# Attention layer with quantised feed-forward: the mask and the maximum of the scores move from TensorE and a plain reduction to a masked reduction on DVE, and DVE's order within a turn changes

## The reference

```
x = x + layernorm(attention(layernorm(x)))
x = x + layernorm(ffn(layernorm(x)))

attention: 32 query heads of 128, 8 key/value heads (4 query heads share one)
  y     = softmax(mask(rope(q) rope(k)^T / sqrt(128))) v     in blocks of 64 rows, each sees itself and the block before,
                                                             key no more than 64 back; the first block of a sequence sees only itself
  o_lin = gated linear attention: S = S * exp(g_t) + softmax(k)_t v_t^T ;  o_t = softmax(q)_t S ;  g = log_sigmoid(k) / 16
  out   = bf16(0.5 * y + 0.5 * o_lin) Wo
ffn: w1, w2, w3 are first rounded to NF4 (per 64 values: scale by the largest magnitude, round to one of 16 codes, scale back),
     then  (silu(x w1^T) * (x w2^T)) w3^T          with a hidden width of 1376
```

## Time and profile before

| | |
|---|---|
| median of 3 runs | 1959.39 us (1958.69 to 1960.08) |
| the profiled execution, its own time | 1959.31 us |
| its span | 1957.5 us, 42161 instructions |
| busy share of PE, DVE, ACT, POOL | 96%, 73%, 63%, 63% |
| granted clock of PE, mean | 0.99 |
| DMA | 61.43 MB, 31 GB/s over the span |

### The profile page before, as it was taken

One profiled execution on the slowest core, in us unless ns is written; L12 is line 12 of the kernel. 1 busy time (PEld: TensorE's weight loads), 2 busy tenths in 40 slices (PEclk: granted clock), 3 DMA queues, 4 the chain that ended last, 5 costly groups with the idle time before them and its releaser, 6 DMA issues.

```text
span 1957.5 us, 42161 instructions
## 1 busy us (share of the span) xinstructions
PE 1876.3 (96%) x11698; PEld 1252.8 (64%) x11698; DVE 1433.4 (73%) x3926; ACT 1229.4 (63%) x4840; POOL 1235.9 (63%) x1150
## 2 busy tenths in 40 slices
PE   4999999999999999999999999999989979999997
PEld 3667677777777777776777676777666635444443
DVE  6998888888888888888888888888899644302022
ACT  5777777777777777777777777776666535312121
POOL 3777777777777777777777777777677521212121
PEclk8999999999999999999999999999999989999999
DMA  5000000000000000000000000000100042000000
GB/s 199 25 26 25 26 25 24 24 24 24 32 25 24 24 24 24 29 24 24 24 24 24 30 29 24 24 24 13 54 13 7 7 134 79 26 1 22 0 21 21
DMA packets 44353, 61.43 MB, mean 31 GB/s; under 512 B 4928, under 2 KB 18496, under 8 KB 44288
## 3 DMA queue, kind: packets, MB, share of 16 engines
q1 hardware_dynamic: 44288, 60.64, 9.6%
HBM read 47.97 MB, written 12.65 MB: 31 GB/s over the span
## 4 chain that ended last, share of the span: by engine, by line
PE 62%; DVE 16%; issue 14%; POOL 3%; ACT 2%; DVEq 1%; DMA 0%; SPq 0%; POOLq 0%; ACTq 0%
PE bank L1250 18%; PE bank L1239 8%; PE bank L1278 6%; PE bank L1221 4%; PE bank L1294 4%; PE bank L1315 4%; PE bank L1379 3%; PE bank L1287 3%; DVE f_s L963 2%; PE bank L1205 2%; PE bank L1304 2%; POOL hl L527 2%; DVE f_nrm L953 2%; PE bank L1270 1%; PE bank L1297 1%
## 5 line engine op out<-in xcount | busy, mean ns | idle before, releaser
L488 POOL TENSOR_TENSOR f_acc<-f_acc,f_s 128x512 f32<-128x512 f32 (+1 forms) x416 | 534.3, 1284 | 30.6 <-POOL f_acc L488 0.4
L1250 PE MATMUL bank<-wh,xh 128*128 (+2 forms) x1024 | 334.9, 327 | 7.3 <-DVE cumh L1099 6.2
L1250 PE MATMUL bank<-wl,xh 128*128 (+2 forms) x1024 | 335.0, 327 | 0.0
L1250 PE MATMUL bank<-wh,xl 128*128 (+2 forms) x1024 | 334.7, 327 | 0.0
L469 POOL TENSOR_TENSOR pr<-pr,rp 128x512 f32<-128x512 f32 x128 | 133.0, 1039 | 229.5 <-DVE rp L894 229.5
L963 DVE TENSOR_SCALAR f_s<-f_nrm 128x512 f32<-128x512 f32 (+1 forms) x480 | 240.9, 561 | 3.7
L575 ACT ACTIVATE qe<-bank,nqm 128x128 f32<-128x128 f32 x512 | 180.8, 365 | 80.3 <-DVE qs L823 57.2
L527 POOL TENSOR_TENSOR hl<-hf,hh 128x512 f16<-128x512 f32 (+1 forms) x44 | 50.8, 1155 | 283.7 <-ACT hh L754 283.7
L1379 PE MATMUL bank<-xh,w 128*128 (+3 forms) x704 | 224.8, 382 | 3.8 <-ACT sg L748 3.8
L603 ACT ACTIVATE pr<-bank,pmx 128x128 f32<-128x128 f32 x512 | 180.9, 367 | 37.5 <-DVE pmx L887 29.6
L1239 PE MATMUL bank<-wh,oT 128*128 (+1 forms) x512 | 194.0, 379 | 3.8 <-DVE xl L1019 1.4
(11 more groups left out here) (177 smaller groups left out, 4973.7 us busy)
## 6 DMA issues: line engine op xcount, KB each, us to landing
f_raw<-wf SPq DMA_DIRECT2D x30, 256.0 KB, 2.6
dequantised<-f_dq SPq DMA_DIRECT2D x30, 256.0 KB, 2.0
wt<-dequantised SPq DMA_DIRECT2D x30, 256.0 KB, 3.0
raw_qkv<-wq SPq DMA_DIRECT2D x29, 256.0 KB, 2.5
raw_o<-wo SPq DMA_DIRECT2D x29, 256.0 KB, 2.6
rows<-x SPq DMA_DIRECT2D x4, 1024.0 KB, 9.3
xr<-x SPq DMA_DIRECT2D x16, 256.0 KB, 3.6
out<-yo SPq DMA_DIRECT2D x16, 256.0 KB, 2.1
```

The source lines that it names most:

```text
L488: nc.gpsimd.tensor_tensor(f_acc[:, 0:w], f_acc[:, 0:w], f_s[:, k % 8, 0:w], ALU.add)\
L1250: last = nc.tensor.matmul(dst, av, w[:, sl + c, lo:hi], start=(n == 0), stop=(n == 3 * NC - 1))
```

## The change

1. **Mask.** PE's mask matmul goes; the first product of the scores opens the bank. `p_max` on DVE is now a memset of one unused column (`pause`), and for each of the four heads an operation that adds the mask to 128 columns of SC, negates them, writes them back and keeps the minimum in `pmx`. ScalarE's exponential gets `scale=-1`. In p=0 the first two heads take the mask from `win0`, which ScalarE copies once per step (`head_mask`).
2. **State.** `state` is split: the sum stays ahead of `p_max`, the scaling stands behind it. `em` (p=1) is now an exponential on ScalarE.
3. **Order.** `rks` moves from ahead of `kt` to behind `log_decay`. The compares (and `f_nrm`) stand ahead of `gl` in all four p; in p=0 they stood behind `use_q`. `nf4_blocks` works one piece ahead, in p=1.
4. **Split of the compares.** 2, 3, 5 and 5.

```diff
-NF4_STEPS = (range(0, 2), range(2, 6), range(6, 11), range(11, 15))
+NF4_STEPS = (range(0, 2), range(2, 5), range(5, 10), range(10, 15))
...
+            def head_mask(t):
+                if t.p == 0:
+                    nc.scalar.activation(win0[:], win[:, t.i % 2, 0:P], ACT.Copy).then_inc(s["head_mask"], 1)
...
                 nc.scalar.activation(edT[:, r, :], SM[:, P:P + 130], ACT.Exp)
+                if t.p == 0 and not (isinstance(t.i, int) and t.i == 0):
+                    nc.scalar.activation(em[:, 0, :], SM[:, 2 * P:2 * P + 1], ACT.Exp,
+                                         bias=keep[:].unsqueeze(2)[:, t.i % 2, :])
...
-                                                bias=pmx[:, r, j:j + 1],
+                                                bias=pmx[:, r, j:j + 1], scale=-1.0,
...
+            def k_sums(t):
+                r = t.p % 2
+                wait_tile(dve, s["ke_ev"], t)
+                nc.vector.reciprocal(rks[:, r, :], ksum[:, r, :]).then_inc(s["rks_d"], 1)
...
             def p_max(t):
                 r = t.p % 2
                 wait_tile(dve, s["sc_done"], t)
-                nc.vector.tensor_reduce(pmx[:, r, :], SC[:].rearrange("p (h n) -> p h n", h=GRP), AX.X, ALU.max,
-                                        negate=True).then_inc(s["pmx_d"], 1)
+                nc.vector.memset(pause[:], 0.0)
+                for j in range(GRP):
+                    sl = slice(j * P, (j + 1) * P)
+                    mask = win[:, 1, sl] if t.p or j >= 2 else win0[:]
+                    last = nc.vector.tensor_tensor_reduce(SC[:, sl], SC[:, sl], mask, -1.0, -MASKED, ALU.add,
+                                                          ALU.min, pmx[:, r, j:j + 1])
+                last.then_inc(s["pmx_d"], 1)
...
                 if l2.real():
-                    state(l2)
+                    state_sum(l2)
                 if l1.real():
                     p_max(l1)
+                if l2.real():
+                    state_scale(l2)
                 log_decay(t)
+                k_sums(t)
+                if t.p == 0 and isinstance(t.i, int) and t.i == 0:
+                    nf4_blocks(0)
+                nf4(t)
                 low_decay(t)
-                if t.p == 0:
-                    nf4_blocks(t.i)
-                else:
-                    nf4(t)
+                if t.p == 1 and not (isinstance(t.i, int) and t.i == STEPS - 1):
+                    nf4_blocks(t.i + 1)
...
                 if l1.real():
                     gla_q(l1)
-                if t.p == 0:
-                    nf4(t)
...
             def scores(t):
...
-                nc.tensor.matmul(SC[:], identb[:], win[:, 1, :] if t.p else win[:, t.i % 2, :], start=True, stop=False)
+                if t.p == 0:
+                    pe.wait_ge(s["head_mask"], t.i + 1)
...
-                                                start=False, stop=(j == 3))
+                                                start=(j == 0), stop=(j == 3))
```

More of the change, by code:

```diff
@@ L214, in layer @@
         rp = sb("rp", [P, 2, GRP])
+        pause = sb("pause", [P, 1])
+        win0 = sb("win0", [P, P], BF16)
         f_max = sb("f_max", [P, 2, NF4_MAX // BLK])
@@ L245, in layer @@
             kmx_d nkm_a kabs_ev kneg_d krope_d g_d gl_d rks_d kt_d qmx_d nqm_a qrope_d rq_d qt_d pmx_d
-            rp_d pm_d pa_ev su_d em_d sr_d acc_d qrope_p krope_p qn_p pn_p
+            rp_d pm_d pa_ev su_d head_mask sr_d acc_d qrope_p krope_p qn_p pn_p
             wqk_sc wqk_hi wqk_lo wo_sc wo_hi wo_lo w0_hi raw_a raw_b consts z_id
@@ L705, in turn @@
                 k_exps(t)
+                head_mask(t)
                 if n == 0:
@@ L857, in gla_k @@
                 wait_tile(dve, s["ke_ev"], t)
-                nc.vector.reciprocal(rks[:, r, :], ksum[:, r, :]).then_inc(s["rks_d"], 1)
                 wait_tile(dve, s["rks_d"], t)
@@ L905, in merge, with state_sum, state_scale @@
                                                op0=ALU.max, op1=ALU.add).then_inc(s["pm_d"], 1)
-            def state(t):
-                r, nxt = t.p % 2, t.back(-1)
+            def state_sum(t):
+                r = t.p % 2
                 wait_tile(dve, s["u_done"], t)
                 nc.vector.tensor_tensor(su, SM[:, 0:P], sr[:, r, :], ALU.add).then_inc(s["su_d"], 1)
+            def state_scale(t):
+                r, nxt = t.p % 2, t.back(-1)
                 if not nxt.real():
@@ L916, in state @@
                 if nxt.p == 0:
-                    nc.vector.tensor_tensor(em[:, 0, :], scale, keep[:, nxt.i % 2:nxt.i % 2 + 1] if isinstance(nxt.i, int)
-                                            else keep[:].unsqueeze(2)[:, nxt.i % 2, :], ALU.mult).then_inc(s["em_d"], 1)
-                    dve.wait_ge(s["em_d"], nxt.i)
                     scale = em[:, 0, :]
@@ L1485, in constants @@
     cum /= 16.0
-    keep = np.ones((P, 2), np.float32)
-    keep[:, 0] = 0.0
+    keep = np.zeros((P, 2), np.float32)
+    keep[:, 0] = MASKED
     return {"cosc": cos, "sinc": sin, "winmask": win, "causal": cau, "cumsum": cum,
```

## The result

The changed kernel took 2040.1 us (median of 4 runs, 2039.6 to 2041.3), the kernel before, on the same chip, 1959.5 (1958.7 to 1960.1): a ratio of 1.0413 (95% interval 1.0395 to 1.0431). The profiled execution has a span of 2037.8 us. It is slower, as forecast, by 80.6 us where 63 were forecast; 2040 lies in the range. Most of the steps were right, and two things that cost time were not among them: what PE does between two passes of its loop, and drops of its clock.

A forecast was written before the change was run, and what follows sets the result against it. The prediction took PE to set the time of the 128 attention turns. PE's 45.2 us per step plus stands of 0.34, 1.9 and 1.4 gave 48.8 against 46.8; over 32 steps +63 us, 2022 us, range 1985 to 2078.

The forecast's parts named there:

- The maximum, M: DVE's masked maximum in every turn: a memset and four pairs at 0.29, 1.22 us in place of 0.61.
- p=2: Third turn of a step: gl behind five compares ends at 4.30 us, so PE stands 0.34 us.
- rival B: Dearer masked pairs on DVE, 0.29 + 0.20 each: gl 0.8 later every turn, near 2080 us; chance 12%.
- p=3: Fourth turn of a step: five compares meet POOL's additions, gl ends at 5.85 us, PE stands 1.9 us.
- p=0: First turn of a step: f_nrm and two compares wait for POOL's additions, PE stands 1.4 us for gl.
- p=1: Second turn of a step: gl done at 3.59, before 4.00; old wait for kt goes; no stand.
- rival C: POOL's additions blocked in turn by DVE's compares in p=3 and p=0: 1.2 us more per step, 2060 us; chance 8%.
- The sum: One step of four turns: 45.2 + 0.34 + 1.9 + 1.4 = 48.8 us against 46.8, +2.0, times 32 steps.
- The clock: PE's granted clock in the stage of the attention turns, taken as 1.00.
- Rival A: POOL's runs end before the compares begin, before 2.2 us in p=3 and p=0: 45.8 per step, 1928 us; chance 10%.

The follow-up runs named there:

- e1: Changed kernel with gl moved ahead of the compares in all four turns: 2004.5 us.
- e2: Kernel before with gl computed behind the NF4 work of its turn, mask and maximum as before: 2003.3 us.
- e3: Changed kernel with the last 13 of POOL's 14 additions per step cut to 8 columns in place of 512: 1936.9 us.
- e5: Changed kernel with TensorE's own loop over the steps written out, the other engines keeping theirs: 2020.9 us.
- e8: Changed kernel with gl moved ahead of the compares in turn p=3 alone: 2019.4 us.
- e6: Changed kernel with the mask matmul and the plain reduction put back: 2037.3 us.
- e4: Kernel before with the change's masked maximum on DVE and the mask matmul gone, order of waits, gl and compares as before: 1972.2 us.
- e14: e4 with one compare moved from p=3 to p=0, behind the rope of q (split 3, 4, 5, 3): 1947.2 us.
- e5b: Kernel before with TensorE's own loop over the steps written out: 1959.3 us.

## Why the prediction was right, and where it was not

The frame held: PE bounds the turns, the missing matmul makes a clean turn 11.29 (11.285 measured in p=1), and gl behind the NF4 work makes PE stand in p=3 and p=0, because compares do not run beside additions. The place, the engine and the sign are shown by e1, e2 and e3. Term by term:

- **The maximum, M.** Taken as 1.22 with pairs of 0.29; measured 0.94, with pairs of 0.25. The read of the accumulator starts with the next masked operation and costs nothing beyond it, and the memset lies under the first. This is why p=2 stands 0.15 and not 0.34 (0.05 in e5), and why rival B is out.
- **p=3.** Stand forecast 1.9, measured 2.06. To this come 0.92 behind it, the groups and the late L1263, a term that the sum didn't have; about 0.4 of the stand itself is the later restart. The turn is 14.28 at full clock where 13.19 was forecast. e5, without the loop, shows a stand of 1.80 and 13.08.
- **p=0.** Forecast 1.4, measured a stand of 0.84 without a drop (turn 1.0 above 11.29) and none behind one (0.14 above). The step that failed is the end of POOL's run, put at T0+4.5: it was T0+2.9 because turn p=3 was longer. In e5, where p=3 isn't, it is T0+4.5 and the turn 1.7 above; in e8, where p=3 is shorter still, T0+5.35 and 2.3 above.
- **p=1.** Nothing, as forecast; the old wait for kt is gone.
- **POOL, rival C.** The additions took 1.35 and 1.33, as in the earlier trace rows, so POOL is hardly delayed here. The Trainium skill's rule ("SBUF — State Buffer", section "Who interferes with whom") would have each of them wait for the other; for DVE these rows agree, for POOL they don't: in after an addition that had a compare slip in ahead of it took 1.34 where the others took 1.27. Beside f_nrm they do agree: in e5 one addition of five took 1.59 against 1.28 for the others.
- **The sum.** 48.8 forecast per step; 49.29 measured in steps at full clock, 49.47 with the drops, 48.71 in e5. Without the loop the sum agrees within 0.1, and in part by luck: 0.3 too much in p=2 and 0.1 in p=3 cancel 0.3 missing in p=0. With the loop 1.1 is missing in p=3, of which 0.4 too much in p=0 and 0.2 in p=2 hide a good half.
- **The clock.** The sum took it as 1.00. In every second step it halves for 3.41 us, which costs 1.28 in that turn, but 0.85 comes back in the next, because POOL's run is then over before DVE's compares: 5 us in the loop. The three drops outside it add some 4 more if nothing comes back there, by the same 1.28, an estimate. That a stand would bring this was in none of the cases.
- **The 80.6 us.** In the span the loop's 24 steps are 64 us longer, the four steps before it 6, the four behind it 8, and the part behind the turns 3. The sum had 2.0 for each of 32 steps, 48 of it in the loop. The 16 that it missed there are the way back through the loop (13) and the drops (5), less 2 by which the rest was forecast too high. The 3 us of the part behind the turns, which was taken as not touched, stay open.
- **Rival A** (faster, POOL done before the compares) failed on its condition: POOL's run in p=3 ends at 716.90, 4 us into the turn, where it had to be 2.2.

What the clock's fall depends on stays open. It came at twelve of the loop's 24 stands of p=3 in after (stand of 2.06 and groups), in 7 of 24 in e6 (1.65 and groups), in 4 of 24 in e8 (2.11 in p=0, no groups), and in the loop never in e5 (1.80, no groups), e2 (1.38 and groups) or e3 (0.42 and groups). Each is one trace.

## What to carry to other kernels

Once an engine that paces a loop is made to wait, count more than the wait: look for loop ends right behind it, and read the granted clock by stage afterwards. Price such a disturbance over the turn behind it as well: of the 1.28 us that a drop cost here the next turn gave back 0.85, and a mean over all steps hid both. Moving one result ahead of slow work on a full engine can move the stand to the next result of the same row, so sum the whole row up to each of its consumers. Where two engines can't run together, when one starts is worth more than what an instruction costs: one compare moved from under the additions turned a loss of 12.7 us (e4) into a gain of 13.4 (e14).

## What the runs showed of the hardware

- A masked 128-column operation from PSUM with its minimum kept, and the read of it: 0.33 and 0.14 us busy, 0.25 from start to start. The Trainium skill ("VectorE: DVE Perf Modes", section on the TRN2 errata) gives 120 cycles plus the columns from PSUM to SBUF, by estimate 0.26 for the operation alone; this kind writes back to PSUM, and its 0.25 from start to start is within 0.01 of that. Its busy time of 0.33 is not, and neither are gh and the subtract behind it (0.20).
- A DVE instruction of 8 columns waits for a whole addition of POOL like one of 512: f_safe took 0.17 or 1.12. Not every DVE instruction does: the masked operations of p=3 in after ran beside an addition (712.86 to 714.13) at the same 0.25 each, and in e4 f_max, which reads 512 columns, took 0.69 beside one and 0.67 in after, where none runs.
- What PE does between two passes of a loop shows only behind a stand: 0.9 us of matmuls in groups and what follows them, and a restart 0.52 behind gl, where it is 0.26 in the middle of a pass and 0.15 outside the loop. It costs nothing in a kernel where PE never stands there (e5b). e3, e2, e6 and after show the same 1.3 us between their other steps and the last, which leaves the loop.
- The clock granted to PE fell to 1.2 GHz for 3.41 us at a time in the middle of the densest stage, 1.6 us after PE had resumed from a stand of 2 us.
